# Gate operands in f16 halves, and the gate weights and pair rows made inside the convolution's second sweep

## What is computed

```
h   = relu(layernorm(x))
c   = relu(bn2(conv17(relu(bn1(conv1(h.T))))) + h.T).T        # convolution of 17 taps along the nodes
s   = h @ w_se.T + b_se                                        # 3 values per node
A   = exp(-|s_n - s_m|^2) * adj
nmp = A @ relu(h @ w_msg.T + b_msg)
gi  = [c, nmp] @ w_ih.T + b_ih ;  gh = h @ w_hh.T + b_hh
r, z = sigmoid(gi_r + gh_r), sigmoid(gi_z + gh_z) ;  n = tanh(gi_n + r * gh_n)
x1  = x + (1 - z) * n + z * h
h2  = relu(layernorm(x1))
out = x1 + relu(h2 @ W[:256] + (adj @ h2) @ W[256:] + bias)
```

## Time and profile before

| | |
|---|---|
| median of 3 runs | 1956.99 us (1953.46 to 1958.75) |
| the profiled execution | 1950.57 us |
| its span (first to last instruction) | 1948.8 us |
| mean granted PE clock | 0.983 |
| PE busy | 1835.8 us, 94% |
| DVE busy | 1488.0 us, 76% |
| ACT busy | 776.3 us, 40% |
| POOL busy | 448.6 us, 23% |

### The profile page before, as it was taken

One profiled execution on the slowest core, in us unless ns is written; L12 is line 12 of the kernel. 1 busy time (PEld: TensorE's weight loads), 2 busy tenths in 40 slices (PEclk: granted clock), 3 DMA queues, 4 the chain that ended last, 5 costly groups with the idle time before them and its releaser, 6 DMA issues.

```text
span 1948.8 us, 36555 instructions
## 1 busy us (share of the span) xinstructions
PE 1835.8 (94%) x12498; PEld 1388.5 (71%) x12498; DVE 1488.0 (76%) x3314; ACT 776.3 (40%) x1432; POOL 448.6 (23%) x589
## 2 busy tenths in 40 slices
PE   3779999999948999999999999999999999999997
PEld 2566777744426887887887887787787787777875
DVE  5899999922246787787778777877877877877876
ACT  4654444442233333343333333333333333333441
POOL 4411111100022222222222222222222222222221
PEclk9899999999978999999999999999999999999998
DMA  5376675592252232232232222222322322322320
GB/s 209 126 260 233 231 254 198 176 346 104 103 173 95 78 99 74 80 98 71 81 98 71 89 89 71 91 87 71 96 82 71 96 82 71 96 82 71 96 83 17
DMA packets 163713, 229.03 MB, mean 118 GB/s; under 512 B 13420, under 2 KB 110563, under 8 KB 162906
## 3 DMA queue, kind: packets, MB, share of 16 engines
q1 hardware_dynamic: 163656, 228.29, 35.2%
HBM read 138.06 MB, written 90.18 MB: 117 GB/s over the span
## 4 chain that ended last, share of the span: by engine, by line
PE 68%; DVE 1%; ACT 0%; DMA 0%; POOL 0%; issue 0%; POOLq 0%; DVEq 0%
PE ps_rz L1301 27%; PE ps_n L1301 14%; PE ps_l L1301 13%; PE ps_b L1301 9%; PE ps_s L1261 3%; PE ps_d L1516 1%; PE ps_d L1310 1%; DMA rows<-spectra 0%; POOL conv_v L1283 0%; POOL conv_x L1278 0%; ACT conv_y L1272 0%; DVE out_sum L1568 0%; DVE out_sb L1572 0%; DVE update L1481 0%; DVE u_s L1551 0%
## 5 line engine op out<-in xcount | busy, mean ns | idle before, releaser
L892 PE MATMUL m_ps<-big 128*128 128x512 f16 (+1 forms) x1152 | 267.0, 375 | 5.2 <-DVE ysb L803 3.0
L1472 POOL TENSOR_TENSOR x_new<-xin,new 128x256 f32<-128x256 f32 x128 | 108.8, 850 | 684.9 <-ACT new L1465 684.9
L1447 ACT ACTIVATE tanh_rz<-sum_rz,w_scale 128x512 f32<-128x512 f32 x128 | 91.9, 718 | 318.1 <-DVE sum_rz L1438 318.1
L1301 PE MATMUL ps_rz<-w_ih,conv_t 128*128 128x512 f32 x768 | 216.1, 417 | 0.0
L1301 PE MATMUL ps_rz<-w_ih,nmp 128*128 128x512 f32 x768 | 205.2, 402 | 0.7 <-DVE nmp L1394 0.7
L892 PEld LDWEIGHTS m_ps<-big 128*128 128x128 f16 x1152 | 112.0, 98 | 109.2 <-DVE ysb L803 4.0
L1301 PE MATMUL ps_rz<-w_hh,ht 128*128 128x512 f16 x768 | 187.2, 380 | 0.0
L1301 PE MATMUL ps_l<-w_l,h2t 128*128 128x512 f16 x768 | 178.6, 383 | 1.4 <-DVE h2t L1528 1.4
L1301 PEld LDWEIGHTS ps_rz<-w_ih,conv_t 128*128 128x128 f32 x768 | 139.8, 189 | 32.1
L803 DVE SCALAR_TENSOR_TENSOR ysb<-m_ps,ysb 128x512 f16<-128x512 f32 x96 | 66.0, 689 | 117.4 <-ACT ysb L722 117.1
L1301 PEld LDWEIGHTS ps_rz<-w_ih,nmp 128*128 128x128 f32 x768 | 134.7, 188 | 28.4 <-DVE nmp L1394 0.9
(11 more groups left out here) (211 smaller groups left out, 3601.3 us busy)
## 6 DMA issues: line engine op xcount, KB each, us to landing
xin<-in_x SPq DMA_DIRECT2D x128, 256.0 KB, 2.9
spectra<-ysb SPq DMA_DIRECT2D x96, 256.0 KB, 2.0
rows<-spectra SPq DMA_DIRECT2D x64, 384.0 KB, 3.4
x_normed<-xhat SPq DMA_DIRECT2D x64, 256.0 KB, 3.4
h_turned<-ht SPq DMA_DIRECT2D x64, 256.0 KB, 2.6
adj_in<-in_adj SPq DMA_DIRECT2D x64, 256.0 KB, 3.6
ht<-h_turned SPq DMA_DIRECT2D x64, 256.0 KB, 3.2
xhat<-x_normed SPq DMA_DIRECT2D x64, 256.0 KB, 3.0
```

The source lines that it names most:

```text
L892: last = pe.matmul(dest, x_, w_, start=n == 0, stop=n == 11, skip_group_check=True)
L1301: last = pe.matmul(dest, stationary(dl), moving(wl), start=start and n == 0, stop=stop and n == 2, **kw)
L1447: act.activation(tanh_rz[:, i, :], sum_rz[:, i, :], ACT.Tanh, scale=w["scale"][:, 4:5]).then_inc(S["rz_tanh"], 1)
L1472: pool.tensor_tensor(x_new[:, i, :], xin[:, p, i, :], new[:, i, :], ALU.add).then_inc(S["x_new_done"], 1)
```

## The change

- In the gates stage conv_t, adj_t, att_s, msg, nmp, u_s and w_ih become f16 pairs. So that nothing leaves the range of f16, splits of adj, att, u and nmp get a scale: ACT in its activation, DVE by scalar_tensor_tensor with a scale from a tile (adj, att, u) or a constant (nmp). The convolution's result is first written once more by ACT (conv_r, relu and scale) and split from there.
- gate_weights is gone. Its work, with new bounds for the scales, is laid into the second sweep of the convolution, by units: DVE takes the largest absolute value of all 64 adjacency matrices (256 KB each through two buffers of xin), the s values at u = 2 to 7, the sides at u = 26 to 29, transposes at u = 30 to 35, weight loads at u = 36, squares at u = 41 to 44, sums of their columns by PE at u = 45, scales at u = 46 to 52, splits of the weights at u = 52 to 55, biases at u = 56 and 57. POOL clears tiles and does the small scale arithmetic.
- w_ih, w_hh and w_msg come transposed from the host, so that PE doesn't transpose them.
- The first loads of graph 0 (`Early.load_first`) are issued at u = 50; only the normed x (`load_late`) behind the last store. Tiles of the gates stage lie in `big`.

Cut to its core (a line of "..." where something is left out):

```diff
 def convolution_weights(...)
                 dve.tensor_copy(cvec[:, 6:8], V(tmp, 3))
+                then(dve.tensor_tensor(bound[:, 0, :], V(tmp, 2), V(tmp, 8), ALU.mult))
+                then(dve.tensor_scalar(bound[:, 0, :], bound[:, 0, :], sc[:, 0:1], 2.0 * (TAPS * D) ** 0.5,
+                                       ALU.mult, ALU.mult))
+                dve.tensor_tensor(bound[:, 1, :], V(tmp, 3), V(tmp, 3), ALU.mult)
+                then(dve.tensor_tensor(bound[:, 0, :], bound[:, 0, :], bound[:, 0, :], ALU.mult))
+                then(dve.tensor_tensor(bound[:, 0, :], bound[:, 0, :], bound[:, 1, :], ALU.add))
+                dve.tensor_tensor(cvec[:, 9:10], bound[:, 0, 0:1], bound[:, 0, 1:2], ALU.add)
...
 def convolution(...)
+        ADJ_AT = [0] + [1] * 10 + [2] * 14 + [1] * 6 + [2] * 10
+        ADJ_FROM = [sum(ADJ_AT[:u]) for u in range(len(ADJ_AT) + 1)]
...
+        def adj_steps(u):
+            return range(ADJ_FROM[u], ADJ_FROM[u + 1]) if 0 <= u < len(ADJ_AT) else ()
+        def quads(u):
+            return [k for k in range(3 * (u - 30), 3 * (u - 30) + 3) if 0 <= k < QUADS]
...
+        def parts(u):
+            return range(2 * (u - 52), 2 * (u - 52) + 2) if 52 <= u < 55 else ()
...
             @block.sync
+                def load_adj(j):
+                    if j < 2:
+                        sp.wait_ge(xhat_done, graphs)
+                    else:
+                        sp.wait_ge(adj_seen, j - 1)
+                    sp.dma_start(xin[:, j % 2, :, :].rearrange("p h d -> p (h d)"), adj_d[j]).then_inc(adj_loaded[j % 2], 16)
...
                 load_bins(0)
-                for m in range(first - HALF_UNITS, first):
-                    load_filters(m - first + HALF_UNITS)
+                load_biases()
+                for u, m in enumerate(range(first - HALF_UNITS, len(MAIN))):
+                    if u < HALF_UNITS:
+                        load_filters(u)
                     store_y(m)
-                load_bins(1)
-                for m in range(first, len(MAIN)):
-                    store_y(m)
+                    if u == HALF_UNITS - 1:
+                        load_bins(1)
+                    for j in adj_steps(u + 1):
+                        load_adj(j)
+                    for k in quads(u - 1):
+                        store_pairs(k)
+                    if u == 36:
+                        load_weights()
...
+                    if u == 50:
...
+                        early.load_first(sp)
                 for i in range(3):
                     sp.wait_ge(y_stored[i], 16 * (len(MAIN) // 3))
+                early.load_late(sp)
...
             @block.scalar
                 for u, m in enumerate(range(first - HALF_UNITS, len(MAIN))):
                     split_y(m)
...
+                    for k in quads(u):
+                        turned_sides(k)
+                    if 41 <= u < 45:
+                        square(u - 41)
+                    for n in parts(u):
+                        weight_high(n)
                     if 2 <= u < HALF_UNITS + 2:
...
                         negate(u - 2)
...
             @block.vector
+                def adj_max(j):
+                    dve.wait_ge(adj_loaded[j % 2], 16 * (j // 2 + 1))
+                    dve.tensor_reduce(largest[:, j:j + 1], xin[:, j % 2, :, :].rearrange("p h d -> p (h d)"), axis=AXIS.X,
+                                      op=ALU.max, apply_absolute_value=True).then_inc(adj_seen, 1)
...
-                for m in range(first - HALF_UNITS, len(MAIN)):
+                for u, m in enumerate(range(first - HALF_UNITS, len(MAIN))):
                     split_y(m)
+                    for j in adj_steps(u):
+                        adj_max(j)
+                    if u == 2:
+                        s_values()
...
+                    if 26 <= u < 30:
+                        for n in range(4 * (u - 26), min(4 * (u - 26) + 4, len(SIDES))):
+                            place_sides(n)
...
+                    for n in parts(u - 1):
+                        weight_low(n)
...
             @block.tensor
+                for u, m in enumerate(range(first - HALF_UNITS, len(MAIN))):
+                    for part in range(4):
+                        main(m, part)
+                    for k in quads(u):
+                        turn_sides(k)
+                    if u == 44:
+                        spread_largest()
+                    if u == 45:
+                        column_sums()

-def gate_weights(nc, ident, w, cvec, s_all, pair_d, a):
...
+class Early:
+    def load_first(self, sp):
+        sp.dma_start(self.inv[:, :, :], self.inverse_d).then_inc(self.inv_loaded, 16)
+        sp.dma_start(self.rows[:, 0, :, :, :].rearrange("p k l o -> p k (l o)"), self.rows_d[0]).then_inc(self.conv_loaded[0], 16)
...
 def gates(...)
-        conv_t = sb("conv_t", [P, 2, 2, H, N], F32R)
-        adj_t = sb("adj_t", [P, 2, 2, H, N], F32R)
+        conv_r = sb("conv_r", [P, H, N])
+        conv_t = sb("conv_t", [P, 2, 2, H, N], F16)
+        adj_t = sb("adj_t", [P, 2, 2, H, N], F16)
...
         def conv_split_high(act, t, p):
             ready(act, "conv_hl", t)
+            before(act, "conv_low", t)
+            act.activation(conv_r[:, :, :], conv_v[:, :, :], ACT.Relu, scale=w["scale"][:, 7:8]).then_inc(S["conv_rel"], 1)
+            ready(act, "conv_rel", t)
             before(act, "n_done", t, H, 2)
-            act.activation(conv_t[:, p, 0, :, :], conv_v[:, :, :], ACT.Relu).then_inc(S["conv_high"], 1)
+            act.activation(conv_t[:, p, 0, :, :], conv_r[:, :, :], ACT.Copy).then_inc(S["conv_high"], 1)
...
         def adj_split_low(dve, t, p):
             ready(dve, "adj_high", t)
-            dve.tensor_tensor(adj_t[:, p, 1, :, :], adj_in[:, p, :, :], adj_t[:, p, 0, :, :].bitcast(F32),
-                              ALU.subtract).then_inc(S["adj_low"], 1)
+            dve.scalar_tensor_tensor(out=adj_t[:, p, 1, :, :], in0=adj_in[:, p, :, :], scalar=w["scale"][:, 6:7],
+                                     in1=adj_t[:, p, 0, :, :], op0=ALU.mult, op1=ALU.subtract).then_inc(S["adj_low"], 1)
```

More of the change, by code:

```diff
@@ L691, in _ @@
+                then(pool.tensor_tensor(M(5), M(5), power[:, 3:4], ALU.mult))
+                pool.tensor_scalar(Q(9), M(5), 2.0 ** -24, None, ALU.mult).then_inc(scales, 1)
+                pool.wait_ge(main_done, first + 3 * HALF_UNITS)
+                pool.memset(early.pairs_flat, 0.0).then_inc(pairs_cleared, 1)
             @block.scalar
@@ new lines, in bias_sum, with adj_spread @@
+                def bias_sum():
+                    dve.wait_ge(bias_loaded, 80)
+                    bias = w["bias_msg"][:, :]
+                    dve.tensor_tensor_reduce(out=math_row[:, :], in0=bias, in1=bias, scale=1.0, scalar=0.0, op0=ALU.mult,
+                                             op1=ALU.add, accum_out=stat[:, 7:8]).then_inc(spread_made, 1)
+                def adj_spread():
+                    dve.wait_ge(adj_seen, graphs)
+                    then(dve.tensor_reduce(stat[:, 8:9], largest[:, :], axis=AXIS.X, op=ALU.max))
+                    dve.tensor_scalar(diag[:, 0, :], ident[:, :], cvec[:, 9:10], None, ALU.mult)
+                    dve.tensor_scalar(diag[:, 1, :], ident[:, :], stat[:, 8:9], None, ALU.mult).then_inc(spread_made, 1)
@@ new lines, in weight_low, with biases @@
+                def weight_low(n):
+                    src, dest, scale = PARTS[n]
+                    dve.wait_ge(weights_high, n + 1)
+                    dve.scalar_tensor_tensor(out=dest(1), in0=src, scalar=w["scale"][:, scale:scale + 1], in1=dest(0),
+                                             op0=ALU.mult, op1=ALU.subtract).then_inc(weights_low, 1)
+                def biases():
+                    dve.wait_ge(bias_loaded, 96)
+                    then(dve.tensor_tensor(w["bias_rz"][:, :], w["bias_rz"][:, :], bias_hh, ALU.add))
+                    dve.tensor_scalar(w["bias_rz"][:, :], w["bias_rz"][:, :], w["scale"][:, 0:1], None, ALU.mult)
@@ L1122, in _, with spread_largest @@
-                for n, (src, k, o, _, _) in enumerate(banks):
-                    if n >= 4:
-                        pe.wait_ge(low, n - 3)
-                    for kh in range(2):
-                        for t in range(2):
-                            last = pe.transpose(psw[n % 4][:, kh * D + t * P:kh * D + t * P + P],
-                                                src[:, o + t, (k + kh) * P:(k + kh) * P + P], ident[:, :])
-                    last.then_inc(turned, 1)
-def gates(nc, ident, w, cvec, inverse_d, x, adj, y_d, h_d, xhat_d, pair_d, out):
+                def spread_largest():
+                    pe.wait_ge(spread_made, 2)
+                    pe.wait_ge(sides_read, QUADS)
+                    pe.matmul(x_ps[1][:, 0:2 * P], ones_f, diag.rearrange("p c k -> p (c k)"), start=True,
+                              stop=True).then_inc(sums_done, 1)
@@ L1545, in passed_high @@
             for i in range(H):
```

(2 more changed lines are left out.)

671 lines of the change are left out of this document (396 added, 275 removed).

## The result

The median after the change is 1934.15 us (5 runs, 1928.88 to 1939.09); beside it the kernel before took 1953.59 us (5 runs). The ratio is 0.990, with a 95% interval of 0.988 to 0.992. I had forecast 1911 with a range of 1865 to 1942: the sign and the range hold, the gain does not. 46 us were forecast against the runs shown before, 19 came. The profiled execution took 1935.05 us (span 1932.8) where my sum, before its 6.4 us for the median, said 1904.7: 30 us too little.

What follows compares the result with a forecast made beforehand. DVE was taken to bound the first sweep, PE the second sweep and last stage. From 1950.6 us, less 43.9 (gap) and 38 (f16), plus 35 (second sweep), 1 (before the first sweep) and 6.4 (median): 1911, range 1865 to 1942.

Steps and rivals of the forecast that it cites:

- Step 1: Gap between second sweep and last stage: without gate_weights, 48.0 us shrink to a hand-over of about 4.1; gain 43.9 us.
- Step 2: Last stage: f16 operands shorten PE's sets, DVE's 8.5 us stretch stays; period 20.78 to 20.18 us, gain 38 us.
- Rival B: Last stage: PE alone sets the period, gain 64 us for 38; total 1885 us; chance 0.15.
- Rival C: Last stage: operand type doesn't change the matmul rate, period stays 20.78 us; total 1949 us; chance 0.08.
- Step 3: Second sweep of the convolution: the loads and work moved into it give time back, +35 us.
- (a): Sweep's start: bins, biases and adjacency tiles queued with the filters at 0.4 MB per us; +9 us by u = 16.
- (b): Sweep units with two adjacency tiles: two-buffer cycle of 3.4 us against 2.59, +0.8 per unit; 9.6 and 4.2 us.
- (c): load_weights at u = 36 in the sweep: 3 MB queued in front of the tiles of u = 38; +7.5 us.
- (d): PE's own additions in the sweep: transposes +1.5 us, column_sums with one f32 matmul +3.3 us.
- (e): Sweep's s values, sides, scales and weight halves on DVE, ACT and POOL: cost nothing, up to 3 us.
- Rival D: Sweep's two-tile units: PE idles enough to drop its clock, 5.18 us per unit; total 1964 us, slower; chance 0.07.
- Rival A: Second sweep hides nearly all the moved work, +11 us only; total 1887 us; chance 0.20.

## Why the prediction was right in two steps and wrong in the third

**Step 1, the gap: right.** 48.0 to 4.4 us, forecast 4.1. The early loads are 3.3 us of it, shown by the run that undoes them.

**Step 2, the f16 operands: right in mechanism, and nearly in size.** Period 20.18 in the graph shown, the forecast's, and 20.11 in the mean, with PE's sets at 1.29 and 0.66 (a set that starts without its weights loaded ahead 1.47) and the first nmp set released by DVE; the stage gave 41.7 us for 38, and 63 x (20.78 - 20.11) is 42. That DVE sets it was inferred from its 8.5 us without a break, and moving adj_split_low shows it. Rival B fell by this, and its floor was somewhat low: PE alone takes 19.93, not 19.76. Rival C fell by the sets' times. The Trainium skill's page "TensorE: Matmul & The Clock Gate", section "Back-to-back issue gap", gives one gap and says nothing of the operands' type; the f16 rows agree with it, and the f32 pairs' rows of before are 7% longer.

**Step 3, the second sweep: +64.4 for +35. This is the step that failed.** By engine time its sum had 30.3 us of waits of PE (a, b and c), 4.8 of new work and nothing for the clock. Measured were 44.5 us more idle time, 5.9 of new work and 13.9 us more for the same 720 matmuls, most of it at the lower clock. So the waits were half of the miss, and the clock, a term set to nothing, about a third. The terms one by one:

(a) The start, +9 by u = 16, is the worst of the terms. The splits show 18.6 by u = 12 and 27.0 by u = 13, PE's own starts 23.4 at u = 16. The rule behind it, bytes added at 0.4 MB per us with PE waiting only for them, was wrong in that it treats a queue as one sum of bytes. What is lost is also a chain: a small tile or filter lies behind 3 MB, DVE (or ACT) stands for it, and the next tile's load is issued only when that one is done. DVE's first tile of the sweep shows it:

```profile
415.99 0.69 DVE L1070 TENSOR_REDUCE largest<-xin 128x1 f32<-128x512 f32 x1 [13.52 <-DMA xin<-in_adj]
```

How much each part has, the runs say by PE's starts. Just behind load_bins(1) the sweep is 24.3 us behind in the changed kernel (u = 18), 15.3 with four buffers (u = 17: 453.00 less 393.71, against 44.0 before) and 7.6 without tiles (u = 18: 449.43 less 393.13, against 48.7). So about 8 us are the large transfers and the biases, about 8 the tiles' bytes and place in the queue, and about 9 the two buffers with their short lead. My 9 was near the first part alone. Moving the biases away shortened the first hole by 3.1 us and the sweep by nothing, but the biases went in front of other tiles, so that run says little of the rule.

(b) The units of two tiles, +0.8 each. In the first run they were +1.2, because the landing was 3.1 us, not the 2.6 I took between the rows of 2.0 and 2.9. Both rows were medians over stretches of their own, and here two tiles and a row store are in flight at a time. The Trainium skill's page "DMA: Bandwidth & Descriptors", section "Anatomy of one DMA", gives the same 2.6 as an estimate, for DMAs that GpSimd issues; the trace here, where SP issues them, differs from it by that 0.5 too. The twelve units cost 13.0 us in place of 9.6. In the second run DVE's units were longer still, 4.0 us, but PE lost only 1.8 us before the hole of load_weights, in place of 4.2: the units that PE's banks let it run ahead were there, and were used up. So this term was small in its error.

(c) load_weights, +7.5: 12.3 by the splits of u = 36 and 39, 9.36 of it PE's hole, the rest DVE's lag and the clock behind the hole.

(d) PE's own work, +4.8: 5.9 measured. (e) DVE's and ACT's other work, nothing: held in the run without tiles. In the changed kernel it does not. Four side rows, one reduction and one split are 1.4 + 0.7 + 0.7 = 2.8 us of DVE in a unit of 2.59, and DVE came to them three units late from the two-tile units: it split u = 25 at 507.27 when PE was about to start u = 28. The turns of u = 30 need the side rows themselves, with no bank between, and PE waited 4.3 us for them.

**The clock, taken at nothing: about 10 us.** I had asked whether PE's share of busy time in the two-tile units would lower its clock, and said no by the earlier trace rows. It didn't: 1.00 in 465 to 505 at 73% busy. Rival D placed the loss there and fell. But PE also stood still in one piece, which I had in (a) and (c), and behind each such hole stands a lower clock: 0.81, 0.74 and 0.74 in the windows above. The mean of one matmul of the sweep rose from 377 to 392 ns, 10.8 us over 720 of them. The rest of the 13.9 us are ends, no work: twelve matmuls that stand alone show 2.76 us at full clock, and 2.59 in an unbroken row. In the run without tiles and with large transfers taken apart, no hole is left before 492 and the mean is 377 ns again. A step for "after a hole the clock" was missing in a sum that had the holes.

**Rival A** said the sweep hides nearly all. Not as the kernel was written; with four buffers and small pieces 175 us is as near as the runs came, 17 over the old sweep.

## What to carry to other kernels

When a load is moved under work that has room, count the buffers before the bytes: with two buffers the tile's landing and its use make a cycle, and any byte queued ahead lengthens it; the same 16 MB cost 46 us with two buffers and 11 with four and loads issued a unit earlier. If the tile's consumer stands in line ahead of the engine's main work, its wait is the main engine's wait. And price a hole of TensorE at more than its length, for the matmuls behind it ran at a lower clock here.

## What the runs showed that I had not expected

- The DMA engines moved 385 to 415 GB/s for windows of 15 us with PE busy 12.2 to 15.0 of 15.0: TensorE was not slowed by a full queue, only by what waited in it.
- With the queue full a 256 KB tile's landing was 4.4 us, with it two thirds full 3.1. With four buffers neither held PE up; landings of 12 us behind a 3 MB load still did.
- Twice a hole was taken away (the biases, the large transfers with two buffers) and the sweep kept its length to 1 and 6 us. Each time the bytes that made it were queued in front of other tiles, and other holes grew or came. A hole's length isn't what its removal gives while something else waits in the same queue.
